# Mixture-of-experts rows: shares applied when the expert result leaves its bank, gathered rows added by the transfer itself, and a new order of late rows and sums

## The chip, the cores and the metric

The kernel runs on one core of a Trainium2 chip. The core has five engines that work at the same time and meet only at semaphores: TensorE (PE, with its weight loads shown apart as PEld), VectorE (DVE), ScalarE (ACT), GpSimd (POOL) and SyncE (SP). SP and POOL issue the transfers between the chip's main memory (DRAM) and the core's on-chip memory; 16 DMA engines carry them out. The metric is the device time of one execution in microseconds (us).

## What is computed

```python
x2 = einsum('bct,bcd->bdt', x, cond_weights[subjects])      # 64 batches, 64 rows each: 4096 tokens of 512
probs = softmax(x2 @ gate_w.T)                              # 8 experts
top_p, top_i = top_k(probs, 2)
h = silu(x2 @ expert_fc1[e].T) * (x2 @ expert_fc2[e].T)     # 352 hidden columns per expert
y = sum over the two chosen e of top_p * (h @ expert_proj[e].T)
s = silu(x2 @ shared_fc1.T) * (x2 @ shared_fc2.T) @ shared_proj.T     # 1408 hidden columns
out = x + y + sigmoid(x2 @ shared_gate_w.T) * s
```

All values are float32. Each product is made of three passes (high by high, low by high, high by low part), since the operands are split in two.

## The kernel before

The 4096 tokens are 32 tiles of 128 rows. The program has three stretches.

**Front and first shared part, 0 to about 417 us.** The conditioning product, the router and 5 of the 11 shared chunks of 128 hidden columns run in 8 blocks of 4 tiles. In block 5 DVE computes the place of every choice (`choice_slots`, `slot_places`): each expert's rows are packed into 71 half tiles of 128 slots (`HALVES`), and `slot_of` (128 x 2 x 32) holds the slot of each token's first and second choice. `token_of`, the token of each slot, follows two blocks later (`slot_tokens`, line 1575) and sets `routing_done`. `p_top` (128 x 2 x 32) holds the two shares of each token. x plus the shared part so far goes to `partial_rows` in DRAM.

**Experts, about 417 to 897 us.** 39 steps: 32 of two half tiles and 7 of one. For each, POOL copies slot indices to `idx_stage`, drains, and gathers 128 token rows per indirect transfer (`gather_rows`, line 761). PE makes the products, ACT copies the finished banks unchanged to `res` (`keep_y`, line 1291) and SP stores them to `slot_rows`. The very first rows are turned by PE (line 854) after row 1 of the last shared block.

**Late part, about 897 us to the end.** The other 6 shared chunks, in 4 blocks of 8 tiles (`HBLOCKS`), each block in two teams of 3 chunks. A chunk is 7 products of 6 matmuls each (`late_product`, line 1126, in the order P1, P6, P7, P5, P2, P4, P3, a scheme that saves an eighth of them). DVE and ACT combine them: lines 1805, 1808, 1811, 1815 and 1818, then the gate and the splits (1798, 1822, 1827, 1829); each line waits for the one before or for ACT. After the three chunks of a team PE makes 8 late rows of 9 matmuls (line 864), alternating between two banks, so that row r may start only when DVE has added row r - 2 into the result (`late_row`, line 1839, semaphore `o_kept`). The result rows of a block are loaded from `partial_rows` in two halves of four tiles (line 553; the first half is `res`, the second `rawp`).

The expert rows come in here. Per tile POOL copies two index columns, drains and gathers the two chosen expert rows from `slot_rows` into `rows` (`gather_slots`, lines 781 and 784), at most two tiles ahead of DVE, which multiplies each by its share and adds it to the result (`late_pick`, line 1792, two instructions a tile). The picks of a block are spread: one in the third chunk of team 0, four between its late rows, three in the chunks of team 1. The four sums that prepare the next block's x (`late_sum`, line 1772) stand behind the chunks of team 1, two of them in front of its first late row.

## Time and profile before

| | us |
|---|---|
| median of 3 runs | 1300.14 |
| lowest, highest | 1299.24, 1305.26 |
| the profiled execution, whole | 1301.66 |
| its span in the trace | 1299.5 |
| PE busy | 1260.2 (97%) |
| DVE busy | 865.5 (67%) |
| ACT busy | 488.9 (38%) |
| POOL busy | 293.1 (23%) |

PE is busy nearly throughout, so the time can fall only where PE waits or where its clock is down; everything else matters as far as it makes PE wait. The matmuls are pipelined: one of 512 columns starts 0.227 us after the one before when nothing holds it, though its record lasts 0.39 us.

### The profile page before, as it was taken

To read this page: it belongs to the slowest core of one execution; us is meant where nothing else is said; L and a number is where in the kernel's file an instruction comes from. 1 tells how busy PE (TensorE), PEld (TensorE's weight loads), DVE (VectorE), ACT (ScalarE), POOL (GpSimd) and SP (SyncE) were. 2 spreads that over 40 slices of the span, in tenths; PEclk is the share of its full clock that TensorE was granted. 3 is DMA by queue.
4 is the path that set the end of the run, shared out by engine and by line. 5 is a ranking of instruction groups with operands and counts; after the bars stand their busy time and mean duration, and the time that the engine had idled before them with its cause. 6 is when DMAs were issued, how large, how long until landed. Compare 5 with 4: busy or idle time off the path is not lost.

```text
span 1299.5 us, 20327 instructions
## 1 busy us (share of the span) xinstructions
PE 1260.2 (97%) x7006; PEld 1079.0 (83%) x7006; DVE 865.5 (67%) x1410; ACT 488.9 (38%) x821; POOL 293.1 (23%) x431
## 2 busy tenths in 40 slices
PE   6999999999999999999999999999998998998998
PEld 5878888888888999999999999998776776786876
DVE  5544444459645777687778777787677667678675
ACT  4322231121012666566666665554223213213211
POOL 4576671000001212212222121100130131031030
PEclk9999999999999999999999999999999999999999
DMA  9597866201234777767767867675965864864852
GB/s 318 190 322 277 291 212 241 105 33 65 98 125 155 274 258 268 259 239 279 266 225 269 289 224 254 248 270 191 335 205 176 267 195 162 263 217 156 269 158 104
DMA packets 110670, 284.29 MB, mean 219 GB/s; under 512 B 11570, under 2 KB 11698, under 8 KB 104850
## 3 DMA queue, kind: packets, MB, share of 16 engines
q1 hardware_dynamic: 96738, 229.25, 50.0%
q0 software_dynamic: 13872, 54.27, 13.4%
q8 instruction: 34, 0.56, 0.2%
q14 instruction: 26, 0.21, 0.1%
HBM read 217.16 MB, written 66.32 MB: 218 GB/s over the span
## 4 chain that ended last, share of the span: by engine, by line
PE 79%; issue 10%; DVE 5%; DMA 2%; POOL 2%; ACT 1%; POOLq 1%; SPq 0%; DVEq 0%
PE bank_h L864 41%; PE bank_o L864 24%; PE bank_h L1126 4%; PE bank_t L1126 3%; PE bank_t L854 2%; POOL rows L784 2%; PE bank_t L864 1%; DMA xf_transposed<-xt 1%; PE bank_t L811 1%; POOLq L782 1%; PE bank_o L821 1%; ACT h_hi L1177 1%; DVE rawp L1792 1%; DVE raw L1818 0%; DVE raw L1827 0%
## 5 line engine op out<-in xcount | busy, mean ns | idle before, releaser
L864 PE MATMUL bank_h<-x_hi,w_hi 128*128 128x256 f32 (+2 forms) x1096 | 349.5, 319 | 4.4 <-DVE x_lo L1655 2.6
L864 PE MATMUL bank_h<-x_hi,w_lo 128*128 128x256 f32 (+2 forms) x1096 | 343.4, 313 | 0.0
L864 PE MATMUL bank_h<-x_lo,w_hi 128*128 128x256 f32 (+2 forms) x1096 | 342.7, 313 | 0.0
L864 PE MATMUL bank_o<-wp_hi,h_hi 128*128 128x512 f32 (+1 forms) x565 | 234.3, 415 | 23.1 <-DVE res L1839 15.4
L864 PE MATMUL bank_o<-wp_lo,h_hi 128*128 128x512 f32 (+1 forms) x565 | 231.4, 410 | 0.0
L864 PE MATMUL bank_o<-wp_hi,h_lo 128*128 128x512 f32 (+1 forms) x565 | 229.9, 407 | 0.0
L864 PEld LDWEIGHTS bank_h<-x_hi,w_hi 128*128 128x128 f32 (+1 forms) x1096 | 201.0, 183 | 16.8 <-issue 5.5
L864 PEld LDWEIGHTS bank_h<-x_hi,w_lo 128*128 128x128 f32 (+1 forms) x1096 | 201.0, 183 | 12.6
L864 PEld LDWEIGHTS bank_h<-x_lo,w_hi 128*128 128x128 f32 (+1 forms) x1096 | 201.1, 183 | 11.2
L1695 DVE TENSOR_TENSOR w_lo<-raw,w_hi 128x704 fp32r<-128x704 f32 x156 | 132.5, 886 | 55.4 <-ACT w_hi L1177 55.4
L864 PEld LDWEIGHTS bank_o<-wp_hi,h_hi 128*128 128x128 f32 (+1 forms) x565 | 107.9, 191 | 53.5 <-DVE res L1839 20.6
L864 PEld LDWEIGHTS bank_o<-wp_hi,h_lo 128*128 128x128 f32 (+1 forms) x565 | 107.7, 191 | 26.0
L1177 ACT ACTIVATE w_hi<-raw 128x704 fp32r<-128x704 f32 (+1 forms) x168 | 126.7, 803 | 3.2 <-DVE raw L1772 3.0
L864 PEld LDWEIGHTS bank_o<-wp_lo,h_hi 128*128 128x128 f32 (+1 forms) x565 | 107.8, 191 | 23.2
L757 POOL COPY idx_stage<-token_of 128x2 int32 (+3 forms) x39 | 9.0, 230 | 505.8 <-PE bank_t L854 322.6
L1223 ACT ACTIVATE g_sb<-bank_h 128x512 f32<-128x512 f32 x40 | 23.9, 598 | 250.8 <-PE bank_h L864 250.8
L1581 DVE TENSOR_TENSOR h_sb<-bank_h,g_sb 96x256 f32<-96x256 f32 (+1 forms) x136 | 68.0, 500 | 60.1 <-ACT g_sb L1223 37.4
L761 POOL DMA_INDIRECT rows<-xf_rows,idx_stage x71 | 86.2, 1214 | 58.9 <-issue 58.9
L784 POOL DMA_INDIRECT rows<-slot_rows,idx_stage x64 | 65.6, 1025 | 107.0 <-issue 107.0
L1422 DVE COPY xt<-bank_t 128x512 f32<-128x512 f32 x28 | 19.4, 692 | 99.6 <-PE bank_t L811 76.0
L1296 ACT ACTIVATE g_sb<-bank_h 128x256 f32<-128x256 f32 (+1 forms) x96 | 36.8, 384 | 112.0 <-PE bank_h L864 112.0
L854 PE MATMUL bank_t<-cst,rows 128*128 128x128 f32 x284 | 75.8, 271 | 0.0
(222 smaller groups left out, 2023.1 us busy)
## 6 DMA issues: line engine op xcount, KB each, us to landing
raw<-ew SPq DMA_DIRECT2D x39, 1408.0 KB, 7.3
rawp<-ewp SPq DMA_DIRECT2D x39, 512.0 KB, 7.9
w_early<-late_up SPq DMA_DIRECT2D x72, 256.0 KB, 3.7
slot_rows<-res SPq DMA_DIRECT2D x32, 512.0 KB, 4.6
x_hi<-late_up SPq DMA_DIRECT2D x48, 256.0 KB, 3.5
x_lo<-late_up SPq DMA_DIRECT2D x48, 256.0 KB, 4.2
xt_in<-xf_transposed SPq DMA_DIRECT2D x11, 1024.0 KB, 7.5
late_up<-raw POOLq DMA_DIRECT2D x6, 1792.0 KB, 7.7
```

What stands on the lines that cost most here:

```text
L761: pool.indirect_dma_start(rows[:, s, :], None, xf_dram, bass.IndirectOffsetOnAxis(idx_stage[:, s:s + 1].bitcast(U32), 0),).then_inc(ex.row ...
L782: pool.drain()
L784: pool.indirect_dma_start(picks[:, u, k, :], None, slot_dram, bass.IndirectOffsetOnAxis(idx_stage[:, 2 * u + k:2 * u + k + 1].bitcast(U32) ...
L854: m = pe.transpose(bank_t[r % 2][:, k * P:(k + 1) * P], source[:, k * P:(k + 1) * P], ident)
L864: mm = pe.matmul(dst, a, m, start=(first and i == 0), stop=(last and i == 2))
L1126: m = pe.matmul(bank[:, :], halves[w][:, k, :], x2[x][:, k, :], start=(first and k == 0 and i == 0), stop=(k == 1 and i == 2), skip_group_ ...
L1177: copy = lambda o, i: nc.scalar.activation(o, i, ACT.Copy)
L1223: nc.scalar.activation(g_sb[:, (j % 2) * BN:(j % 2 + 1) * BN], bank_h[2 * (j % 2)][:, :], ACT.Silu).then_inc(f.g_ready, 1)
L1296: nc.scalar.activation(g_sb[0:fn, j * TS:(j + 1) * TS], bank_h[j][0:fn, 0:TS], ACT.Silu).then_inc(ex.g_ready, 1)
L1422: nc.vector.tensor_copy(xt[:, k % 2, :, :], bank[:, :].rearrange("p (k t) -> p k t", k=KC)).then_inc(fxt_ready, 1)
L1581: nc.vector.tensor_tensor(h_sb[0:fn, g], bank2, g_sb[0:fn, g], ALU.mult).then_inc(f.h_mul, 1)
L1695: nc.vector.tensor_tensor(lo, raw, hi, ALU.subtract).then_inc(ex.w_lo, 1)
```

## The change

1. **Shares by slot.** A new DRAM table `slot_shares` has one number for each slot. POOL clears it, then writes `p_top` into it by 64 indirect transfers of 128 single numbers each, at places `share_at` that DVE computes in one added instruction in `slot_places`. They stand before POOL's wait for `routing_done`. After the first two `gather_rows` POOL waits for the 64 and loads the table as `share_of` (128 x 71).
2. **Weighed when kept.** ACT's copy of an expert bank takes the slot's share as its scale (`weigh`). ACT waits once for `shares_in` before the first expert gate.
3. **Added by the transfer.** `gather_slots` and `late_pick` are gone. POOL now waits for a loaded half of the result, issues four indirect transfers with `compute_op=add` that add the first choices of four tiles directly into it, waits for them (`picked_in[0]`), and issues four for the second choices. DVE's first late row of each half in team 0 waits for `picked_in[1]`. There is no index copy and no drain.
4. **Order of late rows.** PE makes rows 0 and 1 interleaved, the last chunk's parts of both behind the parts of the first two chunks.
5. **Order of sums.** `late_sum` 0 stands before the first chunk of team 1, 1 and 2 before the second, 3 before the third; none stands in front of the rows.

```diff
@@ POOL, after all_xf_stored
+            nc.gpsimd.memset(share_of[:, :], 0.0).then_inc(share_zero, 1)
+            pool.wait_ge(share_zero, 1)
+            shares = share_dram.rearrange("(p n) c -> p (n c)", p=P)
+            nc.gpsimd.dma_start(shares, share_of[:, :]).then_inc(share_cleared, 16)
+            pool.wait_ge(share_cleared, 16)
+            pool.wait_ge(share_places, 1)
+            for k in range(2):
+                for t in range(TILES):
+                    c = k * TILES + t
+                    pool.indirect_dma_start(share_dram, bass.IndirectOffsetOnAxis(share_at[:, c:c + 1].bitcast(U32), 0),
+                                            p_top[:, k, t:t + 1], None).then_inc(shares_sent, 16)
             pool.wait_ge(routing_done, 1)
...
             for u in range(2):
                 gather_rows(u, u, 2 * u)
+            pool.wait_ge(shares_sent, 16 * CHOICES)
+            nc.gpsimd.dma_start(share_of[:, :], shares).then_inc(shares_in, 16)
...
-            def gather_slots(t):
-                u = t % 2
-                at_least(pool, picked_used, t - 1)
-                nc.gpsimd.tensor_copy(idx_stage[:, 2 * u:2 * u + 2], slot_of[:, :, t:t + 1].rearrange("p a b -> p (a b)"))
-                pool.drain()
+            def add_slots(b, half):
+
+                n = 2 * b + half + 1
+                pool.wait_ge(late.res_in[half], 16 * (b + 1))
                 for k in range(2):
-                    pool.indirect_dma_start(picks[:, u, k, :], None, slot_dram,
-                                            bass.IndirectOffsetOnAxis(idx_stage[:, 2 * u + k:2 * u + k + 1].bitcast(U32), 0),
-                                            ).then_inc(picked_in[u], 16)
+                    if k:
+                        pool.wait_ge(picked_in[0], 16 * BT * n)
+                    for r in range(BT * half, BT * (half + 1)):
+                        t = HROWS * b + r
+                        pool.indirect_dma_start(late_res(r), None, slot_dram,
+                                                bass.IndirectOffsetOnAxis(slot_of[:, k, t:t + 1].bitcast(U32), 0),
+                                                compute_op=ALU.add).then_inc(picked_in[k], 16)
@@ ACT
+            weigh = lambda o, i, share: nc.scalar.activation(o, i, ACT.Copy, scale=share)
...
-                    copy(res[:, 2 * u + r, :], bank_o[r][:, :]).then_inc(ex.o_kept, 1)
+                    weigh(res[:, 2 * u + r, :], bank_o[r][:, :], share_of[:, bass.ds(2 * q + r, 1)]).then_inc(ex.o_kept, 1)
...
+            act.wait_ge(shares_in, 16)
@@ DVE
+                nc.vector.scalar_tensor_tensor(out=share_at[:, :], in0=lo_i[:, :], scalar=float(HALVES), in1=hi_i[:, :],
+                                               op0=ALU.mult, op1=ALU.add).then_inc(share_places, 1)
...
                 if g == 0 and r % BT == 0:
-                    dve.wait_ge(late.res_in[r // BT], 16 * (b + 1))
+                    dve.wait_ge(picked_in[1], 16 * BT * (2 * b + r // BT + 1))
```

PE at the start of the late rows of block 0, team 0, before. `bank_o0` and `bank_o1` are the banks of rows 0 and 1 (then 2 and 3); each three matmuls are one chunk's part.

```order
L864 MATMUL bank_o0<-wp_hi,h_hi 128x512 [waits late_h_lo,ex_o_kept,late_wp_in0]
L864 MATMUL bank_o0<-wp_lo,h_hi 128x512
L864 MATMUL bank_o0<-wp_hi,h_lo 128x512
L864 MATMUL bank_o0<-wp_hi,h_hi 128x512 [waits late_h_lo]
L864 MATMUL bank_o0<-wp_lo,h_hi 128x512
L864 MATMUL bank_o0<-wp_hi,h_lo 128x512
L864 MATMUL bank_o0<-wp_hi,h_hi 128x512 [waits late_h_lo]
```

And with the change:

```order
L882 MATMUL bank_o0<-wp_hi,h_hi 128x512 [waits late_h_lo,ex_o_kept,late_wp_in0]
L882 MATMUL bank_o0<-wp_lo,h_hi 128x512
L882 MATMUL bank_o0<-wp_hi,h_lo 128x512
L882 MATMUL bank_o1<-wp_hi,h_hi 128x512
L882 MATMUL bank_o1<-wp_lo,h_hi 128x512
L882 MATMUL bank_o1<-wp_hi,h_lo 128x512
L882 MATMUL bank_o0<-wp_hi,h_hi 128x512 [waits late_h_lo]
```

The wait for the third chunk's low part stood before the 7th matmul and now stands before the 13th; the wait of row 2 for DVE is before the 19th in both.

POOL in the late part of the program, the first tiles, before:

```order
L781 COPY idx_stage<-slot_of 128x2 [waits y_stored0,y_stored1,ex_t_done,ex_rows0]
L784 DMA rows<-slot_rows,idx_stage 128x512 x2
L781 COPY idx_stage<-slot_of 128x2
L784 DMA rows<-slot_rows,idx_stage 128x512 x2
L781 COPY idx_stage<-slot_of 128x2 [waits picked_used]
```

And with the change, one block:

```order
L805 DMA res<-slot_rows,slot_of 128x512 [waits late_res_in0]
L805 DMA res<-slot_rows,slot_of 128x512 x3
L805 DMA res<-slot_rows,slot_of 128x512 [waits picked_in0]
L805 DMA res<-slot_rows,slot_of 128x512 x3
L805 DMA rawp<-slot_rows,slot_of 128x512 [waits late_res_in1]
L805 DMA rawp<-slot_rows,slot_of 128x512 x3
L805 DMA rawp<-slot_rows,slot_of 128x512 [waits picked_in0]
L805 DMA rawp<-slot_rows,slot_of 128x512 x3
```

POOL no longer waits for DVE, but for the loaded half and for its own first four transfers.

DVE between the first and the second chunk of team 1, before (`raw12` holds the intermediate results, and in part the sums):

```order
L1829 TENSOR_TENSOR h_lo<-raw12,h_hi 128x512 [waits late_h_hi]
L1772 TENSOR_TENSOR xt<-picked 128x1024 [waits late_x_in1,late_x_in0]
L1805 TENSOR_TENSOR raw12<-bank_t1,raw12 128x512 [waits late_p1_kept,late_p_full]
L1808 TENSOR_TENSOR raw12<-bank_h0,raw12 128x512 [waits late_u2,late_p_full]
L1811 TENSOR_TENSOR raw12<-bank_h1,raw12 128x512 [waits late_u3,late_p_full]
L1792 SCALAR_TENSOR_TENSOR rawp<-rows,p_top,rawp 128x512 [waits picked_in0]
```

And with the change:

```order
L1849 TENSOR_TENSOR h_lo<-raw12,h_hi 128x512 [waits late_h_hi]
L1805 TENSOR_TENSOR picked<-picked,xt_in 128x4x256 [waits late_x_sums]
L1805 TENSOR_TENSOR raw12<-picked 128x1024 [waits late_x_sums]
L1827 TENSOR_TENSOR raw12<-bank_t1,raw12 128x512 [waits late_p1_kept,late_p_full]
L1830 TENSOR_TENSOR raw12<-bank_h0,raw12 128x512 [waits late_u2,late_p_full]
L1833 TENSOR_TENSOR raw12<-bank_h1,raw12 128x512 [waits late_u3,late_p_full]
```

Two sums stand there instead of one, and the pick behind is gone; in line numbers of the change 1805 is the sum and 1827 what was 1805.

## Rows read from the trace of the kernel before

**Rows 1.** PE's waits from 893 us on: us in total, times, longest

```profile
PE bank_o L864 <- DVE res L1839: 15.4, 8, 3.4
PE bank_o L864 <- DVE h_lo L1822: 5.3, 8, 1.3
PE bank_o L864 <- DVE rawp L1839: 2.2, 2, 1.8
PE bank_h L1126 <- DVE raw L1811: 0.6, 1, 0.6
```

**Rows 2.** Timeline of PE, first waits: start us, us, what, idle before and releaser

```profile
927.05 0.39 PE L864 MATMUL bank_o<-wp_hi,h_hi 128*128 128x512 f32 x1
932.94 0.50 PE L864 MATMUL bank_o<-wp_hi,h_hi 128*128 128x512 f32 x1 [1.03 <-DVE res L1839]
945.54 0.56 PE L864 MATMUL bank_o<-wp_hi,h_hi 128*128 128x512 f32 x1 [1.78 <-DVE rawp L1839]
...
977.89 0.39 PE L864 MATMUL bank_o<-wp_hi,h_hi 128*128 128x512 f32 x1
986.51 0.57 PE L864 MATMUL bank_o<-wp_hi,h_hi 128*128 128x512 f32 x1 [3.43 <-DVE res L1839]
987.30 0.63 PE L864 MATMUL bank_o<-wp_hi,h_lo 128*128 128x512 f32 x1
987.73 0.63 PE L864 MATMUL bank_o<-wp_hi,h_hi 128*128 128x512 f32 x1
...
1187.98 0.64 PE L864 MATMUL bank_o<-wp_hi,h_hi 128*128 128x512 f32 x1 [3.42 <-DVE res L1839]
```

**Rows 3.** Stretches of PE: us, busy (count), granted clock, DMA share, GB/s

```profile
927.00:933.00 6.00, 4.65 (x20) 1.00 0.90 292
945.50:949.50 4.00, 3.96 (x10) 0.57 0.43 131
```

**Rows 4.** Timeline of DVE at the end of the last chunk, teams 0 and 1

```profile
932.14 0.74 DVE L1839 SCALAR_TENSOR_TENSOR res<-bank_o,s_gate,res 128x512 f32<-128x512 f32 x1
...
983.32 1.22 DVE L1772 TENSOR_TENSOR raw<-picked 128x1024 f32<-128x1024 f32 x1
985.71 0.74 DVE L1839 SCALAR_TENSOR_TENSOR res<-bank_o,s_gate,res 128x512 f32<-128x512 f32 x1
```

**Rows 5.** Loads of the result halves: SP's issues, then lowest, median, highest to landing

```profile
901.93 0.39 SPq L553 DMA_DIRECT2D res<-partial_rows  x1
997.53 0.38 SPq L553 DMA_DIRECT2D res<-partial_rows  x1
DMA to landing us min/median/max: 5.3/5.5/8.5
```

**Rows 6.** Stretches with the DMA share: us, POOL busy (count), clock, DMA share, GB/s

```profile
905.00:920.00 15.00, 2.49 (x4) 1.00 1.03 391
1029.00:1044.00 15.00, 4.00 (x6) 1.00 0.75 246
```

**Rows 7.** The gathers of expert rows, line 784, and their landing

```profile
L784 POOL DMA_INDIRECT rows<-slot_rows,idx_stage x64: 946/969/1858, 903.1 to 1266.1; - x64
DMA to landing us min/median/max: 3.3/4.5/8.0
```

**Rows 8.** The gathers of tokens, line 761: the first two, then all (page)

```profile
385.57 1.04 POOL L761 DMA_INDIRECT rows<-xf_rows,idx_stage  x1 [2.87 <-issue]
386.91 0.97 POOL L761 DMA_INDIRECT rows<-xf_rows,idx_stage  x1 [0.30 <-issue]
...
L761 POOL DMA_INDIRECT rows<-xf_rows,idx_stage x71 | 86.2, 1214 | 58.9 <-issue 58.9
```

**Rows 9.** The first tokens: DVE's slot places, PE's turning of the first rows

```profile
305.25 0.19 DVE L1553 TENSOR_SCALAR raw<-slot_of 128x64 int32<-128x64 int32 x1
408.40 1.03 PE L854 MATMUL bank_t<-cst,rows 128*128 128x128 f32 x8
```

**Rows 10.** DMA in the first 4 us: packets, MB, then the queue's share of 16 engines

```profile
DMA packets 1000, 0.26 MB, mean 64 GB/s; under 512 B 996, under 2 KB 996, under 8 KB 1000
...
q1 hardware_dynamic: 1000, 0.26, 31.1%
```

More of the change, by code:

```diff
@@ L1170, in _ @@
                             pe.wait_ge(ex.o_kept, 2 * XT)
-                    for r in range(HROWS):
-                        late_row(b, g, r)
+                    late_rows(b, g)
         @block.scalar
@@ L1811, in late_chunk @@
                 nc.vector.tensor_tensor(h2_sb, bank_h[1][:, :], u3_sb, ALU.add).then_inc(late.c22, 1)
-                if pick is not None:
-                    late_pick(pick)
                 dve.wait_ge(late.p_full, at + P4)
```

98 lines of the change are left out of this document (48 added, 50 removed).

## Prediction, made before the changed kernel was run

> **What bounds the kernel now.** PE does: it is busy 97% of the span. So I read first what PE waits for, then the timeline around each wait, then what the engine named was doing. All of PE's waits that the change touches lie after 893 us, in the late part [rows 1]. There are three kinds, and the reader should see each in [rows 2].
>
> At the start of the late rows, eight times, PE waits twice: for the last chunk's low part (5.3 us in all) and, before row 2, for DVE's sum of row 0 (15.4 us in all). The second wait is 1.03 us in five of the eight and 3.4 in three, those of team 1 in blocks 0 to 2. [rows 4] show why: two sums for the next block (983.32 to 985.71) stand ahead of DVE's first row.
>
> Between late rows, twice, PE waits 2.2 us in all, 1.78 of it before row 7 of block 0: DVE picked expert rows there and had waited for their gather.
>
> The third kind is the clock. After the wait of 1.78 us the granted clock averages 0.57 over 4 us [rows 3], so PE is mostly at 1.2 instead of 2.4 GHz. After that of 3.43 us matmuls follow each other by 0.43 us (987.30, 987.73 in [rows 2]) instead of 0.227, for some 8 matmuls: 8 x 0.2 = 1.6 us. This happens four times: in block 0 as said, and after the three waits of 3.4 us. In the joint with 1.03 us the clock stays at 1.00 [rows 3].
>
> **Part by part, on the profiled execution (span 1299.5 us, whole 1301.7 us).**
>
> *Picks leave DVE.* 64 tiles x 2 x 0.75 us is 96 us less DVE work, but nearly all ran beside PE. What it frees on the path: 2.2 us of waits between rows, one fall of the clock (1.6), and waits inside block 1's chunks, 0.6 [rows 1] and about as much again in slower restarts and a like wait for ACT. I take 2.2 + 1.6 + 1.2 = **-5.0 us**.
>
> *Sums leave the joint.* Row 2 of team 1 starts 986.51 - 977.89 = 8.6 us after row 0; in team 0 it is 932.94 - 927.05 = 5.9 us. The 2.7 us between them are the 2.4 us of sums and 0.3 us for which a pick delayed the chain. In blocks 1 and 2 the same pick delays it by about 1.0 us: 3.4 us each. Together **-9.5 us**, and if the clock stays up, 3 x 1.6 = **-4.8 us**. The sums go where DVE has room; only two in a row ahead of the second chunk bring line 1811 too late for the last product, by my count by 0.2 us: 3 x 0.2 = **+0.6 us**.
>
> *Interleaved rows 0 and 1.* I give this **nothing**. The low part is there when PE gets to it now, but row 2 still waits for DVE, whose chain from the last product to the sum of row 0 (932.14, [rows 4]) doesn't start a moment earlier. Two waits become one, of 5.9 us less 18 x 0.227 = 4.1 us and the tail of the last matmul: 1.6 us. That lies between 1.03 (clock up) and 1.78 us (clock down). 1.78 was one case, 1.03 five without a fall; between them I take 2 falls in 8: **+3.2 us**, with 0 and 12.8 as ends.
>
> *The additions.* They need the loaded half first, and DVE's first row now needs the additions. The trace has no adding transfer; the nearest is the plain gather: 0.97 us to issue, a gap of 0.30 [rows 8], 4.5 us to landing in the middle, 3.3 to 8.0 at the ends [rows 7]. A group of four then takes 3 x 1.27 + 4.5 = 8.3 us, at the ends 7.1 and 11.8. A half is two groups with a wait between; the other half's first group is issued 5.1 us after the second group starts.
>
> Block 0: the load is issued at 901.93 and takes up to 8.5 us [rows 5], since the DMA engines are full (share 1.03, [rows 6]): 910.4. Group 1, also in the full stretch, 11.8: 922.2. Group 2 is in by 930.5, in time for DVE's first row at 932.1. Group 3 starts at 927.3 and meets the next x and the down weights, so 10: 937.3. Group 4: 945.6. DVE needs it for row 4 by 940.3, so that PE can start row 6 on time (932.94 + 8.2 us, less the sum's 0.75). Late by **+5.3 us**, and the clock falls then, **+1.6 us**.
>
> Blocks 1 to 3: the load is issued at 997.53 and lands by 1003.3; the last group is in at 1008.4 + 3 groups. At 8.3 that is 1033. It is needed at 1042.4: row 2 of block 1 follows that of 986.51 after six rows (12.3), the slow clock (1.6), three chunks (126 x 0.227 = 28.6) and 5.9 us, at 1034.9, and 8.2 less 0.75 us are added as above. Nothing is lost up to 11.3 us a group. I take **0**. The DMA share there is 0.75 [rows 6], so there is some room but not much. If every group took 7.1 us, as with the shortest gathers, block 0 would not be late either; if a group took twice 8.3 us, it would be late by 25 us, and blocks 1 to 3 by 16 us each.
>
> *Shares by slot.* DVE's places are ready at about 305.7 (one added instruction after 305.25, [rows 9]); POOL has nothing to do then until the routing is done, shortly before its first gather at 385.57 [rows 8]. 64 x 1.27 = 81 us, plus 2.9 us of first use as in [rows 8]: 389.8. The first gather is then issued 5 to 10 us later than now, if the drain before it waits for the last small transfers too (I allow 4.5 us), and lands by 400 to 406. PE needs it at 408.40 [rows 9]. **0**, with 2 to 8 us to spare. The table's load follows the second pair of gathers, at about 405, and ACT wants it only after the last two shared rows of 15 matmuls, at 416: 0. The gathers that follow wait for PE, as now.
>
> The 64 write single numbers. 996 packets under 512 B took 31.1% of 16 engines over 4 us at the start [rows 10], 0.02 us each, so 64 x 144 cost 12 us of all engines, spread over 81. By the Trainium skill (DMA: Bandwidth & Descriptors, Specifications) transfers below 512 B make the engine read, modify and write; no row here shows such writes into DRAM.
>
> *ACT's scale.* The copy has the same shape with a scale per partition. ACT is busy 38%, and no wait of PE in the expert part names it: 0.
>
> Sum: -5.0 - 9.5 - 4.8 + 0.6 + 3.2 + 5.3 + 1.6 = -8.6 us. 1301.7 - 8.6 = 1293.1 for a profiled execution; the median of the runs is 1.5 us below that scale: 1291.6, say **1291.5 us**.
>
> **Rivals.**
>
> *The additions are the new bound (slower).* An adding transfer reads the row and the place it goes to. If that doubles the landing, a group is 3.8 + 9.0 = 12.8 us. Block 0 is then in at 910.4 + 5.1 + 38.4 = 953.9, late by 13.6; blocks 1 to 3 at 1046.8, late by 4.4 each, 13.2 in all; the clock falls in each, 6.4. Instead of +6.9 that is +33.2: -8.6 + 26.3 = +17.7, **1317.8 us**. It decides from about 11.3 us a group, where blocks 1 to 3 begin to be late. For it: a full DMA in block 0, and 16 transfers a block crowded into the 40 us before the rows need them, which are now spread over the whole block of 100 us. Against it: POOL's pace of 1.27 us leaves the engines time. The Trainium skill speaks for it (Collectives: The Full Stack, The bandwidth ceiling): a reducing transfer runs at about half the rate of a copy because it needs two source reads. No row here has one.
>
> *The clock falls at every joint (no change).* Eight single waits of 1.6 us instead of pairs: 12.8 instead of 3.2 us: +9.6, **1301 us**.
>
> *The shares come late (no change).* The mean of all token gathers is 1.214 us [rows 8], not 0.97. At 1.51 us apiece the 64 take 97 us, the first rows land at about 416, PE stands 7.5 us and its clock falls: +9.1, **1300.6 us**. It decides from 1.39 us apiece.
>
> *Nothing is late and the clock holds (faster).* -8.6 - 3.2 - 5.3 - 1.6: **1281.5 us**.
>
> **How the numbers follow.** Forecast 0.42, additions bind 0.25, clock at every joint 0.11, shares late 0.10, all in time 0.12. The range must leave out no more than 0.2: 1281 to 1318. A measurement tells 0.5%, 6.5 us, from no change: below 1293.6 is faster, above 1306.6 slower. The forecast lies 2 us inside faster, so a tenth of it goes to same: faster 0.48, same 0.25, slower 0.27.
>
> **What would show it.** In the changed profile: one wait of 1.6 us before row 2 in all eight joints, and no sums ahead of it; no wait before row 7; in block 0 a wait of DVE before row 4 of about 5 us for the adding transfers and none in blocks 1 to 3; the first token gather issued by 395 us and no wait of PE at 408; two clock falls at joints. Wrong it would be if DVE waits for the additions in every block, if the 64 take over 89 us, or if landing of an addition is beyond 7.5 us.

## The result, and the profile of the changed kernel

The changed kernel is slower: **1343.0 us** (median, 1342.8 to 1345.3) against 1301.3 us, ratio 1.032, 95% interval 1.030 to 1.034. Its profiled span is 1343.3 us (before 1299.5). The forecast was 1291.5 us with a range up to 1318.

To see where the time went I took one event of PE that both traces have: the first hidden product of the last expert tile but one. In the kernel before it is this row:

```profile
871.04 0.28 PE L864 MATMUL bank_h<-x_hi,w_hi 128*128 128x256 f32 x1
```

and after the change this one:

```profile
881.12 0.28 PE L882 MATMUL bank_h<-x_hi,w_hi 128*128 128x256 f32 x1
```

The spans differ by 43.8 us. So 10.1 us are lost before this event and 43.8 - 10.1 = 33.7 us after it, nearly all of that in the late part. PE's waits from 893 us on, to be read against [rows 1] (total, times, longest):

```profile
PE bank_o L882 <- DVE rawp L1858: 22.1, 4, 12.8
PE bank_h L1144 <- DMA w_early<-late_up: 14.5, 3, 5.4
PE bank_o L882 <- DVE res L1858: 12.6, 8, 1.6
PE bank_t L1144 <- DMA w_early<-late_up: 4.8, 1, 4.8
```

The third row is the joint, and it is as forecast: one wait in place of two, of 1.6 us, eight times. The first is DVE waiting for additions ahead of row 4, in **every** block. The second and fourth were on nobody's list: the weights of a chunk's first products (w_early) are late, once in each block. In the kernel before, PE waited for them once, and hardly:

```profile
PE bank_h L1126 <- DMA w_early<-late_up: 0.2, 1, 0.2
```

Timeline of PE at the first ones (start, duration, wait), against [rows 2]:

```profile
932.29 0.77 PE L1144 MATMUL bank_t<-x_hi,w_early 128*128 128x512 f32 x1 [4.78 <-DMA w_early<-late_up]
...
949.19 0.50 PE L882 MATMUL bank_o<-wp_hi,h_hi 128*128 128x512 f32 x1 [1.58 <-DVE res L1858]
...
970.48 0.80 PE L882 MATMUL bank_o<-wp_hi,h_hi 128*128 128x512 f32 x1 [12.81 <-DVE rawp L1858]
...
1041.54 0.77 PE L1144 MATMUL bank_h<-w_hi,w_early 128*128 128x512 f32 x1 [4.59 <-DMA w_early<-late_up]
```

The granted clock tells short waits from long ones (stretch, busy and count, clock, DMA share, GB/s), as in [rows 3]:

```profile
920.00:930.00 10.00, 7.46 (x32) 1.00 1.03 279
970.00:974.00 4.00, 3.52 (x8) 0.50 0.00 0
1012.00:1016.00 4.00, 3.84 (x17) 1.00 0.00 0
1041.00:1045.00 4.00, 3.46 (x9) 0.57 1.01 356
```

Behind the joint waits of 1.6 us (here 1012) the clock stays at 2.4 GHz. Behind 12.8 and 4.6 us PE runs at 1.2 GHz. The first row shows what happens to the weights: the DMA engines are full (share 1.03) but move 279 GB/s. In the kernel before, with a share as high, they moved 391 [rows 6]. SP issues the weights in question at the same point of the program; here before, then after:

```profile
908.76 3.52 SPq L536 DMA_DIRECT2D w_early<-late_up  x3
```

```profile
919.05 3.04 SPq L541 DMA_DIRECT2D w_early<-late_up  x3
```

The issue is 10.3 us later, as PE itself is. Before, PE started on this chunk 8.8 us after that issue (917.53) without a wait; now it starts 13.2 us after it (932.29), 4.8 us of them waiting. So the transfer takes longer, and isn't sent later.

POOL in block 0, from the landing of the loaded half on. The bracket is POOL's idle time:

```profile
918.95 1.71 POOL L805 DMA_INDIRECT res<-slot_rows,slot_of  x1 [49.70 <-DMA res<-partial_rows]
...
933.97 1.53 POOL L805 DMA_INDIRECT res<-slot_rows,slot_of  x1 [7.65 <-DMA res<-slot_rows,slot_of]
...
941.33 1.54 POOL L805 DMA_INDIRECT rawp<-slot_rows,slot_of  x1 [0.30 <-issue]
...
958.22 1.54 POOL L805 DMA_INDIRECT rawp<-slot_rows,slot_of  x1 [9.41 <-DMA rawp<-slot_rows,slot_of]
```

An addition is issued in 1.54 us and 0.30 of gap, where a gather took 0.97 [rows 7], and POOL then stands 7.7 to 9.4 us until its group of four has landed. A group takes 933.97 - 918.95 = 15.0 us, the third 16.9, in the later blocks 14.4 to 15.2; the forecast had 8.3.

The 10 us ahead of the late part begin here. POOL's index copy right behind the last small transfer, and the first gather, against 385.57 in [rows 8]:

```profile
399.06 0.20 POOL L773 COPY idx_stage<-token_of 128x2 int32<-128x2 int32 x1
407.39 1.01 POOL L777 DMA_INDIRECT rows<-xf_rows,idx_stage  x1 [8.13 <-issue]
```

In this execution PE was late already by then. From 393 to 402 us it stood up to 1.5 us between matmuls without a releaser, and its granted clock was 0.57 from 402 to 407 us:

```profile
399.76 0.59 PE L882 MATMUL bank_h<-x_lo,w_hi 128*128 128x512 f32 x1 [1.46 <-issue]
```

### The profile page after: what moved, and what is told of

It is laid out like the page before. It is cut to its first block, busy times and chain, and to the rows that moved or that the text cites. A ratio compares the mean times of both kernels' runs of the same rounds, so it can differ in the third digit from the quotient of the medians.

```text
span 1343.3 us, 20271 instructions
## 1 busy us (share of the span) xinstructions
PE 1269.4 (94%) x7006; PEld 1087.0 (81%) x7006; DVE 820.9 (61%) x1347; ACT 493.3 (37%) x821; POOL 388.7 (29%) x466
## 4 chain that ended last, share of the span: by engine, by line
PE 74%; DMA 12%; POOL 6%; DVE 4%; issue 3%; ACT 1%; SPq 0%; POOLq 0%; ACTq 0%; DVEq 0%
PE bank_h L882 38%; PE bank_o L882 22%; DMA rawp<-slot_rows,slot_of 5%; PE bank_h L1144 5%; PE bank_t L1144 4%; POOL res L805 3%; POOL rawp L805 3%; DMA res<-slot_rows,slot_of 3%; PE bank_t L872 2%; DMA res<-partial_rows 2%; PE bank_t L882 2%; DMA out<-res 1%; PE bank_t L829 1%; DMA rawp<-ewp 1%; PE bank_o L839 1%
## 5 line engine op out<-in xcount | busy, mean ns | idle before, releaser
L882 PEld LDWEIGHTS bank_h<-x_hi,w_hi 128*128 128x128 f32 (+1 forms) x1096 | 202.0, 184 | 18.7 <-issue 6.8
L882 PEld LDWEIGHTS bank_h<-x_lo,w_hi 128*128 128x128 f32 (+1 forms) x1096 | 202.0, 184 | 13.2 <-issue 1.9
L805 POOL DMA_INDIRECT res<-slot_rows,slot_of x32 | 49.6, 1549 | 274.3 <-DMA res<-partial_rows 235.9
L766 POOL DMA_INDIRECT slot_shares<-p_top,share_at x64 | 72.7, 1135 | 96.8 <-DVE share_at L1585 77.6
L777 POOL DMA_INDIRECT rows<-xf_rows,idx_stage x71 | 81.6, 1149 | 58.0 <-issue 58.0
```

Of the source, the lines that this page charges most:

```text
L766: pool.indirect_dma_start(share_dram, bass.IndirectOffsetOnAxis(share_at[:, c:c + 1].bitcast(U32), 0), p_top[:, k, t:t + 1], None).then_in ...
L777: pool.indirect_dma_start(rows[:, s, :], None, xf_dram, bass.IndirectOffsetOnAxis(idx_stage[:, s:s + 1].bitcast(U32), 0),).then_inc(ex.row ...
L805: pool.indirect_dma_start(late_res(r), None, slot_dram, bass.IndirectOffsetOnAxis(slot_of[:, k, t:t + 1].bitcast(U32), 0), compute_op=ALU. ...
L882: mm = pe.matmul(dst, a, m, start=(first and i == 0), stop=(last and i == 2))
```

## The experiments

Theory: the additions are slow in themselves, and they crowd out the weights; the shares come late. "Late part" below is the kernel's lag behind the kernel before (its profile) at the end of the span, less its lag at the event at 871.04. In the nine kernels whose code up to there is that of the kernel before, the event lies at -1.6 to +4.0 us, so its column is good to a few us; the late part's is steadier (+33.7 and +33.1 for the same kernel). Median and ratio are from the timed runs, each against its own runs of the kernel before.

| run | median us | ratio (95%) | lag at 871.04 | late part |
|---|---|---|---|---|
| changed kernel | 1343.0 | 1.032 (1.030 to 1.034) | +10.1 | +33.7 |
| after_again | 1342.9 | 1.033 (1.032 to 1.035) | +5.5 | +33.1 |
| a_no_adds | 1285.8 | 0.989 (0.987 to 0.991) | +4.2 | -20.4 |
| a_plain | 1302.9 | 1.001 (0.999 to 1.002) | +10.3 | -6.0 |
| a_regroup | 1316.8 | 1.012 (1.010 to 1.014) | +6.4 | +8.9 |
| a_no_shares | 1339.5 | 1.030 (1.028 to 1.032) | -1.2 | +34.8 |
| a_52_shares | 1337.1 | 1.029 (1.027 to 1.030) | -0.2 | +36.7 |
| a_regroup_no_shares | 1312.5 | 1.009 (1.007 to 1.011) | +3.3 | +9.1 |
| a_hold | 1349.3 | 1.037 (1.035 to 1.040) | +13.8 | +38.3 |
| o_rows | 1301.1 | 1.000 (0.999 to 1.002) | -0.9 | 0.0 |
| o_sums | 1292.8 | 0.993 (0.992 to 0.995) | -1.6 | -9.6 |
| o_both | 1295.1 | 0.994 (0.992 to 0.996) | +0.5 | -5.3 |
| o_both_late_pick | 1296.2 | 0.996 (0.995 to 0.998) | -1.5 | -5.0 |
| o_sums_picks | 1311.9 | 1.010 (1.008 to 1.011) | -0.7 | +8.4 |
| o_direct | 1293.5 | 0.994 (0.993 to 0.996) | +4.0 | -8.4 |
| o_sums_direct | 1288.5 | 0.990 (0.987 to 0.993) | +0.5 | -13.6 |
| o_sums_picks_direct | 1285.3 | 0.986 (0.983 to 0.989) | +2.9 | -15.2 |
| o_in_rows_direct | 1284.0 | 0.987 (0.984 to 0.990) | +0.2 | -17.9 |

### The additions

**a_no_adds**: no additions.

```diff
-            for b in range(HBLOCKS):
-                for half in range(2):
-                    add_slots(b, half)
...
-                    dve.wait_ge(picked_in[1], 16 * BT * (2 * b + r // BT + 1))
+                    dve.wait_ge(late.res_in[r // BT], 16 * (b + 1))
```

> The changed kernel without its 64 adding transfers; the expert rows are therefore not added to the result, and DVE's first late row of a half waits for the loaded half instead. All the rest stays: shares by slot, ACT's scale, both orders. Theory (the additions are what slows the late part, by their waits and by what they do to other transfers): the waits for rawp L1858 (22.1 us) and for w_early (19.3 us) both go, the eight joint waits of 1.57 us stay without a fall of the clock, the stall of 9.2 us near 394 us stays: about 1291 us (the sum of the prediction with all in time, 1281.5, and the stall). Rival (the weights come late because of the new order of sums or rows, not because of the additions): PE's waits for w_early stay at 15 to 19 us, about 1310 us.

1285.8 us, 5 us below the theory's 1291, which had counted a stall of 9.2 us near 394 us that this profile doesn't have. PE's waits in the late part:

```profile
PE bank_o L879 <- DVE res L1855: 12.6, 8, 1.6
PE bank_h L1141 <- DMA w_early<-late_up: 1.9, 3, 1.3
```

The waits for w_early fall from 19.3 to 1.9 us with the additions, so it isn't the new order of sums or rows that makes the weights late; the rival falls. The additions cost 33.7 + 20.4 = 54 us of the late part (57 us between the medians).

**a_plain**: the same transfers without the addition.

```diff
-                                                compute_op=ALU.add).then_inc(picked_in[k], 16)
+                                                ).then_inc(picked_in[k], 16)
```

> The changed kernel with its 64 adding transfers made plain gathers of the same rows into the same places, with the same waits; the loaded result and the first choice are overwritten instead of added to, so a part of the sum is left out. Theory (an adding transfer costs the DMA engines and POOL more than a gather: in the changed kernel 1.84 us apart instead of 1.27, and 90 engine-us per MB instead of 50): a group of four takes about 8 to 9 us instead of 16, block 0 is late by about 5 us, blocks 1 to 3 are in time, the waits for w_early are under 4 us in all: 1301 us (forecast of the prediction plus the stall of 9.2 us). Rival (the crowding of 16 transfers into the time before the rows, and the wait for a group to land, cost the time, whatever the transfer does): over 1325 us.

1302.9 us. In the late part -6.0 us, so 40 of the 54 us are the adding itself. The queue of POOL's transfers over 70 us of block 0 (packets, MB, share of 16 engines), changed kernel:

```profile
q0 software_dynamic: 2304, 4.20, 33.8%
```

and with plain gathers:

```profile
q0 software_dynamic: 1280, 4.20, 17.0%
```

The same sixteen transfers and bytes: 0.338 x 16 x 70 / 4.20 = **90 engine-us per MB** for additions, 0.170 x 16 x 70 / 4.20 = **45** for gathers, and 144 packets a transfer instead of 80. The Trainium skill (Collectives: The Full Stack, The bandwidth ceiling) has a reducing transfer at about half a copy's rate, because it needs two source reads. By that rule, the trace agrees: the factor here is 2.0 in the engines' time. Here is the answer of PE's waits to the forecast, which had priced additions as gathers:

```profile
PE bank_o L882 <- DVE res L1858: 12.6, 8, 1.6
PE bank_h L1144 <- DMA w_early<-late_up: 6.4, 3, 2.4
PE bank_o L882 <- DVE rawp L1858: 3.9, 1, 3.9
PE bank_t L1144 <- DMA w_early<-late_up: 1.0, 1, 1.0
```

One wait for rawp, in block 0, of 3.9 us (forecast 5.3), none in blocks 1 to 3: the schedule of the forecast held for gathers. It held narrowly, since a group of gathers took 10.0 to 11.4 us here and not 8.3, and from 11.3 us on blocks 1 to 3 would be late by the forecast's own sum. And 7.4 us for w_early stand here too (expected: under 4), 1.9 of them in the run without additions; crowding 16 transfers into 40 us costs the rest even with gathers. Priced as gathers, then, the additions would have cost -6.0 + 20.4 = 14.4 us of the late part, where the forecast had 6.9.

**a_regroup**: first choices of both halves, then second choices of both, with a semaphore for each half.

```diff
             for b in range(HBLOCKS):
-                for half in range(2):
-                    add_slots(b, half)
+                for k in range(2):
+                    for half in range(2):
+                        add_group(b, k, half)
```

> The changed kernel with the four groups of a block in another order: first choices of half 0, first choices of half 1, second choices of half 0, second choices of half 1, so that POOL issues while a group lands. Theory A (POOL stands idle 7.7 to 9.4 us twice a block while a group lands, and this makes half 1 late): block 0's last group is in about 13 us sooner, the waits for rawp in blocks 1 to 3 (9.3 us) go, with the falls of the clock: 1316 us. Theory B (the DMA engines are full: share 1.03 to 1.09 wherever additions run beside loads, so an earlier addition only makes another transfer late): PE's waits for rawp shrink, those for w_early grow, 1333 to 1343 us.

1316.8 us, 26 us less: theory A, within 1 us of its number. POOL in block 0 now issues without standing for a landing:

```profile
920.28 1.53 POOL L804 DMA_INDIRECT res<-slot_rows,slot_of  x1 [0.30 <-issue]
923.20 1.90 POOL L804 DMA_INDIRECT rawp<-slot_rows,slot_of  x1 [1.38 <-DMA rawp<-partial_rows]
...
944.44 1.54 POOL L804 DMA_INDIRECT rawp<-slot_rows,slot_of  x1 [0.30 <-issue]
```

Its last addition is issued at 944.44 instead of 963.75. Theory B is wrong on the time, and the waits for w_early don't grow as it says; but they don't go either:

```profile
PE bank_o L882 <- DVE res L1858: 16.0, 8, 5.0
PE bank_h L1144 <- DMA w_early<-late_up: 14.0, 3, 5.1
PE bank_t L1144 <- DMA w_early<-late_up: 1.9, 2, 1.5
```

No wait for rawp is left, but PE still waits 15.9 us for w_early (19.3 before the regrouping). So of the 54 us, 25 were POOL standing while groups landed. Of the other 29, PE's waits account for 18.5 (14 of them for w_early, 3.4 for the first half's additions in block 0), and the granted clock fell to 0.50 to 0.61 behind four of them. That the engines, filled by additions, are the cause of these is argued from their share (1.08 to 1.10 behind these waits) and from the plain gathers' 7.4 us; no run takes a part of the additions away.

### The shares

**a_no_shares**: without the small transfers, the table's clearing and its load; every share is 1.0.

```diff
-            for k in range(2):
-                for t in range(TILES):
-                    c = k * TILES + t
-                    pool.indirect_dma_start(share_dram, ...
...
-            pool.wait_ge(shares_sent, 16 * CHOICES)
-            nc.gpsimd.dma_start(share_of[:, :], shares).then_inc(shares_in, 16)
+            nc.gpsimd.memset(share_of[:, :], 1.0).then_inc(shares_in, 16)
```

> The changed kernel without the 64 small transfers that write the shares by slot and without the table's clearing and loading; every share that ACT scales by is 1.0, so the output lacks the shares. ACT's scaled copy stays. Theory (the small transfers, still running when the first expert weights are loaded, stall PE near 394 us): the stall and the fall of the clock after it go, 9 to 10 us: 1333.5 us. Rival 1 (the stall belongs to something else that changed, such as ACT's scaled copy or a shifted program): it stays, 1343 us. Rival 2 (the expert part was bound by the next wait anyway): half comes back, 1338 us.

**a_52_shares**: 52 of the 64.

```diff
-                for t in range(TILES):
+                for t in range(TILES if k == 0 else 20):
...
-            pool.wait_ge(shares_sent, 16 * CHOICES)
+            pool.wait_ge(shares_sent, 16 * 52)
```

> The changed kernel with 52 of the 64 small transfers: the shares of the last 12 tiles' second choices stay zero, so a part of the output is left out. At 1.43 us apiece 52 take 74 us and end near 382 us, where the routing is done and before the first expert weights are loaded (384.9 us). Theory (the first rows are late because the 64 take 92 us instead of the 81 predicted, and because the drain before the gather lasts 8.1 us behind them instead of 2.9): the first gather is issued by 392 us, PE waits for no row near 408 us: 7 to 10 us less than the changed kernel, 1334 us. Rival (the drain lasts 8.1 us behind any number of them, or PE's place is set by the expert weights): 3 us less or none.

**a_regroup_no_shares**: the edits of a_regroup and a_no_shares together.

> The changed kernel with the groups of additions in the other order (first choices of both halves, then second choices) and without the small transfers; the shares are left out (every one is 1.0). Theory (the two causes lie in different stretches and add up; the regrouped kernel took 1316.8 us): 8 to 9 us less, 1308 us. Rival (what the earlier stretch gives back is taken by full DMA engines in block 0, as the run without shares alone, only 3.5 us faster, may mean): 1313 us.

**after_again**: the changed kernel once more.

> The changed kernel itself once more, on the same chip as the runs beside it. In its first profile PE issued matmuls 1.4 us apart from 393 to 402 us and stood 9.2 us behind the kernel before from then on; in three variants that keep the 64 small transfers PE ran on there and waited 3.1 to 5.6 us for its first rows instead. Theory (the small transfers' lateness costs 7 to 10 us by 890 us in either form): time 1343 us again, and at 893 us PE is 8 to 10 us behind the kernel before, with or without the slow issue at 394 us. Rival (the slow issue is a cost of its own that comes on top in some executions): where it is absent the time is 1336 us.

Without the small transfers, and with 52 of them, PE has no wait between 385 and 420 us and passes the event at 871.04 at -1.2, +3.3 and -0.2 us. With all 64 it passes it at +4.2 to +10.3 in five profiles, in which the transfers take 92 to 94 us; the lowest of these is hardly outside the scatter of the event, but in four of the five PE stands 3.1 to 5.6 us for its first rows, and in the fifth it has the slow issue. The second profile of the changed kernel has no slow issue at 394 us. It has what the forecast's rival described, a late first gather (405.94 us, again behind a drain of 8.13), and PE waits 3.2 us for those rows. The two medians are the same 1343 us, but the two profiled executions took 1345.3 us with the slow issue and 1340.5 without, and their lags at the event, 10.1 and 5.5 us, differ as much. So in that execution it cost about 5 us more than waiting for the rows did; how many of the timed ones have it isn't known. In the timed runs the shares are worth less than at that event: 5.8 us between a_52_shares and after_again on one chip (7 to 10 expected), 4.3 us between the two regrouped kernels (8 to 9 expected, the rival's 1313 us met), 3.5 for a_no_shares (9 to 10 expected). The late part takes 0 to 4 us of it back, as its column shows. Rival 2 of a_no_shares, then, is nearest.

The drain is long behind 52 as well, 9.03 us, as that run's rival had it; the first gather is in time there because it is issued at 392.21 us, 14 to 15 us sooner.

**a_hold**: one more wait of SP.

```diff
+            sp.wait_ge(shares_sent, 16 * CHOICES)
             load_expert(0, 0)
```

> The changed kernel with one more wait: SP loads the first two experts' weights only when the 64 small transfers have landed. Theory A (the drain before the first token gather is 8.1 us long because the DMA engines are full of expert weights, share 0.95 to 1.13 from 388 to 396 us): the drain shrinks to about 3 us, the first gather is issued near 402 us, but the weights now land by 409 to 412, so the time is within 3 us of the changed kernel, 1343 us. Theory B (the small transfers themselves, 128 writes each, take that long to land): the drain stays near 8 us, the weights come later still, 1345 us or more.

1349.3 us: theory B has the times right (a drain near 8 us, over 1345 us), but not its reason. SP's wait ends, all small transfers landed, 3.1 us after the last was through on POOL, yet POOL's drain is 8.13 us as ever:

```profile
401.98 0.20 POOL L774 COPY idx_stage<-token_of 128x2 int32<-128x2 int32 x1
410.32 1.01 POOL L778 DMA_INDIRECT rows<-xf_rows,idx_stage  x1 [8.13 <-issue]
```

```profile
405.08 0.00 SPq L518 DMA_DIRECT2D raw<-ew  x1
```

So the drain is not the landing. Nor is it full engines, theory A's reason: here they fill during the drain, but in the changed kernel's first profile they moved nothing in all of it, and both drains last 8.13 us. The stretches of the drain, the changed kernel's and then this one's from SP's first load on (busy and count, clock, DMA share, GB/s):

```profile
399.30:407.30 8.00, 7.29 (x18) 0.57 0.00 0
```

```profile
405.00:410.30 5.30, 5.18 (x14) 0.57 0.87 316
```

What POOL does in it stays open. PE's slow issue came back in this profile, though the DMA engines stood nearly empty (share 0.01 at 398 to 400 us), so full engines don't cause that either; its cause is open too.

### The orders, and a better kernel

**o_rows**, **o_sums**, **o_both**: the kernel before with the interleaved rows alone, the moved sums alone, and both. **o_both_late_pick** moves DVE's picks from the even to the odd rows besides. PE's edit is `late_rows` of the changed kernel, word for word; DVE's are these (the last two lines only in o_both_late_pick):

```diff
                 for j in range(TEAM):
-                    late_chunk(b * LATE + TEAM + j, HROWS * b + HROWS - TEAM + j)
                     if b + 1 < HBLOCKS:
-                        late_sum(b + 1, j)
-                if b + 1 < HBLOCKS:
-                    late_sum(b + 1, 3)
+                        for q in ((0,), (1, 2), (3,))[j]:
+                            late_sum(b + 1, q)
+                    late_chunk(b * LATE + TEAM + j, HROWS * b + HROWS - TEAM + j)
...
-                    if r % 2 == 0:
+                    if r % 2:
```

> The kernel before with PE's first two late rows interleaved and nothing else. Theory (row 2 waits for DVE's chain in any case): one wait in place of two at each of eight joints, of 1.6 us in five and about 4 us in three, the falls of the clock as before: within 2 us of the kernel before, 1300 us. Rival A (with no wait for the last chunk's low part the clock holds at the three long joints as well): 1295 us. Rival B (DVE's pick between row 0 and row 1 now holds up row 3, since PE finishes row 1 with row 0): eight more small waits, 1304 us.

> The kernel before with one part of the change alone: DVE's four sums for the next block stand ahead of the second team's chunks (one, two, one) instead of the last two at the joint. Picks, plain gathers and row order as before. Theory (the sums at the joint cost three waits of 3.4 us and three falls of the clock): -9.5 - 4.8 + 0.6 us, of which 2.3 us stay because a pick still delays the last chunk: -11.4 us, 1289 us, with three waits before row 2 of team 1 of about 1 us instead of 3.4. Rival (two sums and a pick ahead of or in the second chunk make DVE late inside it): half of it comes back, 1295 us.

> The kernel before with both orders of the change (sums ahead of the chunks, first two rows interleaved), but picks on DVE and plain gathers as before: no additions by transfer and no shares by slot. Theory (the two orders are the whole gain of the change that does not come from the picks; rows give nothing): as the run with the sums alone, 1289 us, all eight joints with one wait of 1.6 us. Rival (the orders only help together with DVE's freed time): 1295 us or more.

> As the run with both orders, and DVE's four picks between the rows of team 0 stand after the odd rows instead of the even ones, so that row 1's sum follows row 0's at once and each gather has one row longer to land. Theory (a pick between rows 0 and 1 holds up row 3 by some 0.2 us, and the pick that waits for its gather costs 1.8 us and a fall of the clock in block 0): 2 to 3 us less than both orders with the picks where they were, 1286.5 us. Rival (the gather's landing sets the time, wherever the pick stands, and the pick after row 7 now delays the next chunk): no difference, 1289 us.

The rows alone do nothing (1.000, interval 0.999 to 1.002), as forecast. The sums alone gain 8.3 us; 11.4 were expected. What is missing stands in their waits:

```profile
PE bank_o L864 <- DVE res L1839: 8.2, 8, 1.0
PE bank_o L864 <- DVE h_lo L1822: 5.9, 8, 1.3
PE bank_h L1126 <- DVE raw L1811: 4.8, 3, 1.8
```

The joints are cured: all eight waits before row 2 are 1.0 us, 15.4 us have become 8.2, and the clock falls behind none of them. But a chunk with a pick and two sums ahead of it is too much for DVE: 4.8 us, where the forecast had 0.6. Without picks (a_no_adds) those waits don't exist.

Both orders together were expected at 1289 us with eight waits of 1.6 us, and took 1295.1, which is the rival's number. The interleaved rows are not quite free here: five waits are 1.6 to 2.0 us, but three are 2.4 us in one piece, where o_sums has 1.3 and 1.0 us apart, and behind each of the three the granted clock is 0.57 to 0.66 over 4 us, where o_sums has 1.00:

```profile
PE bank_o L864 <- DVE res L1850: 15.7, 8, 2.4
```

The medians differ by 2.3 us, and the two intervals overlap. Moving the picks by a row (1286.5 expected) does nothing.

**o_sums_picks** deals the picks out so that none meets two sums: picks 0 and 1 in team 0's chunks 1 and 2, picks 2 to 6 between its rows, pick 7 in team 1's first chunk.

```diff
-                    late_chunk(b * LATE + j, HROWS * b if j == TEAM - 1 else None)
+                    late_chunk(b * LATE + j, HROWS * b + j - 1 if j else None)
...
-                    if r % 2 == 0:
+                    if r % 2 == 0 or r == HROWS - 1:
...
-                        late_pick(HROWS * b + 1 + r // 2)
+                        late_pick(HROWS * b + 2 + (r + 1) // 2)
...
+                    late_chunk(b * LATE + TEAM + j, None if j else HROWS * b + HROWS - 1)
```

> The kernel before with the sums ahead of the second team's chunks (one, two, one) and the picks dealt out anew so that no pick meets two sums or the last chunk of team 1: picks 0 and 1 in chunks 1 and 2 of team 0, picks 2 to 6 between the rows of team 0, pick 7 in chunk 0 of team 1. Row order, gathers and shares as before. Theory (in the run with the sums alone PE waited 4.8 us inside chunks because a pick and two sums met there): those waits go, all eight joints keep 1.03 us: 1287 us, 5 us less than the sums alone (1292.8). Rival (the picks that come sooner wait for their gathers, DVE being late in their place): 1293 us or more.

1311.9 us, **19 us slower** than the sums alone. DVE's first wait, then PE's:

```profile
DVE rawp L1792 <- DMA rows<-slot_rows,idx_stage: 37.8, 16, 4.5
```

```profile
PE bank_h L1126 <- DVE raw L1811: 18.7, 7, 5.3
```

The picks now wait for their gathers. POOL's timeline shows the pace:

```profile
936.07 0.98 POOL L784 DMA_INDIRECT rows<-slot_rows,idx_stage  x1 [2.63 <-issue]
...
938.31 0.19 POOL L781 COPY idx_stage<-slot_of 128x2 int32<-128x2 int32 x1
942.49 0.97 POOL L784 DMA_INDIRECT rows<-slot_rows,idx_stage  x1 [3.99 <-issue]
```

Between the copy of the index and the gather POOL drains, and right behind another pair that takes 3.0 to 4.5 us (7.3 and 5.4 in the full stretch at the start): a pair each 6 us. The changed kernel shows the way out, since its additions take the slot table itself as index. Four kernels use it for plain gathers, and leave copy and drain out:

```diff
-                nc.gpsimd.tensor_copy(idx_stage[:, 2 * u:2 * u + 2], slot_of[:, :, t:t + 1].rearrange("p a b -> p (a b)"))
-                pool.drain()
...
-                                            bass.IndirectOffsetOnAxis(idx_stage[:, 2 * u + k:2 * u + k + 1].bitcast(U32), 0),
+                                            bass.IndirectOffsetOnAxis(slot_of[:, k, t:t + 1].bitcast(U32), 0),
```

**o_direct** has this alone; **o_sums_direct** and **o_sums_picks_direct** add the sums, and the sums and dealt picks. **o_in_rows_direct** leaves the picks where they were and puts two of the four sums after rows 5 and 7 of team 0, one each ahead of chunks 1 and 2 of team 1:

```diff
                         late_pick(HROWS * b + 1 + r // 2)
+                    elif r > 3 and b + 1 < HBLOCKS:
+                        late_sum(b + 1, r // 2 - 2)
...
                 for j in range(TEAM):
+                    if j and b + 1 < HBLOCKS:
+                        late_sum(b + 1, j + 1)
                     late_chunk(b * LATE + TEAM + j, HROWS * b + HROWS - TEAM + j)
```

> The kernel before with one edit: POOL gathers the picked rows with the slot table as index, without the index's copy and the drain. Theory (the two parts are separate: the drain costs the waits before rows 7 and 8 of block 0, 2.2 us, a fall of the clock, 1.6, and some restarts; the joints keep their sums): 1297 us. Rival A (the drain costs nothing while the sums stand at the joint): 1301 us. Rival B (with rows in hand early the picks no longer stand in the chain at the joints, so that these shorten as well): 1292 us.

> The kernel with the sums moved ahead of the chunks, and POOL's picks gathered with the slot table itself as index: no copy of the index and no drain before each pair. Theory (the drain waits for the pair before to land, so a pair takes about 6 us, and DVE's picks wait for it): DVE's waits for the gathered rows shrink from about 11 us to under 4, PE's two waits before late rows in block 0 (2.0 us) and the fall of the clock behind go: 1289 us against 1292.8 for the sums alone. Rival (DVE's own time is what the picks cost): 1292 to 1293 us.

> The kernel with the sums ahead of the chunks and the picks dealt out anew (1311.9 us), with the slot table as index and no drain. Theory (that run was slow because picks 6 and 7 come 2 and 7 us after their forerunners while a pair of gathers took 6 us from drain to drain): DVE's 37.8 us of waits for gathered rows fall to under 10 and PE's 18.7 us for line 1811 to under 3: 1288 us. Rival (the rows land late because of the DMA engines, not the drain): 1305 us or more.

> The kernel before with picks where they were, gathered with the slot table as index and no drain, and the four sums spread differently: two after the odd rows 5 and 7 of team 0, where DVE has 1.3 us to spare, and one each ahead of chunks 1 and 2 of team 1. Row order as before. Theory (in the run with the sums alone the 4.8 us inside chunks come from two sums and a pick in one chunk; with one each there is room): no waits for line 1811, no waits before row 7: 1286 us. Rival (the sums in the rows hold up PE's rows, since the x for the next block is not there in time): waits before rows 6 and 7 in each block, 1293 us.

Copy and drain together were worth 8.0 us, between the theory (1297) and rival B (1292): DVE's waits for gathered rows go from 20.5 to 1.9 us. Rival B's mechanism is not what gave it, since the joints are as long as before (15.4 us in [rows 1]):

```profile
PE bank_o L862 <- DVE res L1837: 15.3, 8, 3.4
```

PE's waits in the late part shrink by 4.0 us in all, and the clock falls at two places instead of four, 3.2 us at the forecast's 1.6 a fall; that is 7.2 of the late part's 8.4 us. One of the two places is the joint of block 2, where the clock held this time behind the same 3.42 us (before it was 0.57):

```profile
1185.30:1189.30 4.00, 4.00 (x18) 1.00 0.00 0
```

With the sums it is 12.6 us, with dealt picks 15.9, so their 19 us loss was the pace of the gathers indeed. **o_in_rows_direct** takes 1284.0 us, ratio 0.987 (0.984 to 0.990), 17 us less than the kernel before and 59 less than the changed one. (The interval of o_sums_picks_direct lies beside it; the two are not told apart.) What PE still waits for in its late part:

```profile
PE bank_o L862 <- DVE res L1837: 8.1, 8, 1.0
PE bank_o L862 <- DVE h_lo L1820: 3.0, 6, 1.0
PE bank_o L862 <- issue: 1.3, 2, 0.6
PE bank_o L862 <- DVE rawp L1837: 1.0, 1, 1.0
PE bank_h L1124 <- DMA w_early<-late_up: 0.8, 1, 0.8
```

## Why the prediction was wrong

**The additions** were the step that failed. Forecast +6.9 us in all, measured 54: 14 for sixteen transfers crowded ahead of the rows, 40 for adding in them. The term took the nearest row, a gather of 0.97 us that lands in 4.5 us, so 8.3 us a group, and set 11.8 as the upper end. Measured: 3 x 1.84 us to the last of the group, 1.54 for it and 7.1 to 9.4 us more until it has landed, 14.4 to 16.9 us. The nearest rows gave no bound, since none of them had an adding transfer, and what an addition costs more stood only in a rival of 0.25. The rival had the right mechanism and too low a price: its landing of 9.0 us was met (1.54 + 7.65 = 9.2), but it left the pace of issue at 1.27 us, where 1.84 was measured. With 14.9 us a group, its own formula gives block 0 late by 910.4 + 5.1 + 44.7 - 940.3 = 19.9 us and blocks 1 to 3 by 1053.1 - 1042.4 = 10.7 each, 52.0 + 6.4 us instead of 33.2: 1317.8 + 25.2 = 1343.0 us. That this meets the measurement is luck, for three reasons. The 5.1 us in it is four issues at 1.27 us; at the measured 1.84 it is 7.4, four times 2.3 us more, and the formula gives 1352 us. Half 0 in block 0, in time by the forecast (930.5 for 932.1), was late too: in the second profile PE stands 5.6 us before row 2 for it, which in the first is hidden behind the weights. And in blocks 1 to 3 PE waited 4.0, 3.9 and 1.4 us for the additions, not 10.7 each, because it was held up before by something else:

**The weights** were missing from the sum. The forecast read the DMA share (1.03 and 0.75, [rows 6]) only as a delay *to* the additions, never as what the additions do to others. PE waited 19.3 us for w_early, and its clock fell to 0.50 to 0.64 behind all four of these waits (4.5 to 5.4 us). With plain gathers it is still 7.4 us. Part of that was to be foreseen: 16 transfers had been moved into a stretch where the engines' share was 1.03.

**Shares by slot**: forecast 0 with 2 to 8 us to spare, measured 4 to 10 us at 871 us and 3.5 to 5.8 in the times. The 64 took 92 to 94 us, not 81 (the median is 0.96 us, as taken, but some take up to 2.8), and the drain 8.1, not 4.5. By the rival's own numbers (97 us, +9.1) this was a fair description at a chance of 0.10. The engines' time was no part of it: between 388 and 405 us 384 packets of the small transfers took 1.7% of 16 engines, 0.012 us each, where the forecast had taken 0.02 from [rows 10]. The Trainium skill (DMA: Bandwidth & Descriptors, Specifications) says that transfers below 512 B are read, modified and written; the trace shows no price for it in the engines' time.

**The sums** leaving the joint: right. -9.5 - 4.8 + 0.6 was forecast for them together with the picks' absence, and in a_no_adds no joint is longer than 1.6 us. The term of 0.6 holds only where picks are gone (0 in a_no_adds, 4.8 us in o_sums).

**Interleaved rows**: right at nothing for the order, and 1.6 us for the wait (eight measured, 1.57 to 1.58). The clock fell behind none of them in the changed kernel's first profile; +3.2 us were forecast for two.

**Picks leaving DVE**: the gains hold as a sum. All in time, the forecast for the late part was -8.6 - 3.2 - 5.3 - 1.6 = -18.7 us; a_no_adds measured -20.4. But -5.0 of it was put down to the work that leaves DVE, and o_direct shows that 8 us can be had without taking a pick from DVE, by leaving out POOL's copy and drain.

**ACT's scale**: 0, right; no wait names it in a_no_shares.

So the gains were sized well, and an operation that the trace had never shown was priced by its nearest relative, at that relative's pace of issue, and without what it takes from the weights beside it.

## What to carry to other kernels

Before work is moved from an engine to the DMA, count what it takes of the DMA engines: an adding transfer here took twice what a gather took, and whoever shared the full stretch paid too, the weights first. Groups of transfers that must follow each other are better interleaved with other groups, so that one lands while the next is issued; that alone was worth 26 us of the 42 here. And look at how a gather gets its index: this kernel copied it to a stage and drained, 3.0 to 4.5 us right behind another pair, and with the table used in place it needed neither.

## What the runs showed that was not expected

- An adding indirect transfer is dearer on POOL as well as on the DMA engines: 1.54 us to issue against 0.95 for the same transfer without the addition, 144 packets against 80, 90 engine-us per MB against 45.
- POOL's drain behind the 64 small writes is 8.13 us in each of six profiles, with the DMA engines empty in it (share 0.00 in five) or filling (0.87 in a_hold), and although in a_hold the writes land within 3.1 us. Behind 52 of them it is 9.03 us, at a share of 0.93.
- PE can stand up to 1.5 us between matmuls, again and again for 9 to 12 us, without a releaser in the trace and with the DMA engines empty (a_hold) or full (first profile of the changed kernel, share 0.90), and not at all in another execution of the same code. The runs don't say why.
